# One tile of rows in every three rounds fetched by SyncE, row by row, and left out of GpSimd's gathers

## The reference

```
s, v = x[:, :64], x[:, 64:].reshape(n, 32, 3)
h_s, h_v = (s @ lin1_ws) * a / 8, einsum('nci,cd->ndi', v, lin1_wv) * a / sqrt(32)
w = silu(edge_scalars @ fc_w1 / 8) @ fc_w2 / 8            # 224 weights an edge
w1..w5 = split(w);  es, ev = h_s[edge_src], h_v[edge_src]  # the gather
messages = products of w1..w5, es, ev and the 4 edge attributes
agg = segment_sum(messages, edge_dst) / 4
out = layernorm(x + gated(sc(x) + lin2(agg)))
```

## Time and profile before

| | us |
|---|---|
| median of 3 runs | 3984.4 (3984.01 to 3986.15) |
| the profiled execution | 3985.22 |
| its span | 3983.4 |
| PE busy | 3715.0 (93%) |
| POOL busy | 2965.0 (74%) |
| DVE busy | 2438.8 (61%) |
| ACT busy | 2019.7 (51%) |

### The profile page before, as it was taken

One profiled execution on the slowest core, in us unless ns is written; L12 is line 12 of the kernel. 1 busy time (PEld: TensorE's weight loads), 2 busy tenths in 40 slices (PEclk: granted clock), 3 DMA queues, 4 the chain that ended last, 5 costly groups with the idle time before them and its releaser, 6 DMA issues.

```text
span 3983.4 us, 63960 instructions
## 1 busy us (share of the span) xinstructions
PE 3715.0 (93%) x18692; PEld 1572.6 (39%) x18692; DVE 2438.8 (61%) x7711; ACT 2019.7 (51%) x5186; POOL 2965.0 (74%) x3149
## 2 busy tenths in 40 slices
PE   7999999999999999999999999999999999999998
PEld 5344433433333433333333333333333333333333
DVE  6666666666656665666666666666666666666665
ACT  3455545554545455545555555555554545454554
POOL 5777777777777777777777777777777777777775
PEclk8999999999999999999999999999999999999999
DMA  7644444444444444444444444444444444444443
GB/s 270 184 131 130 127 127 120 129 123 127 121 126 123 127 123 127 124 127 122 128 122 128 122 128 122 127 122 126 124 123 126 123 127 122 128 121 127 122 128 101
DMA packets 367409, 516.31 MB, mean 130 GB/s; under 512 B 67378, under 2 KB 246266, under 8 KB 366942
## 3 DMA queue, kind: packets, MB, share of 16 engines
q0 software_dynamic: 150384, 256.47, 25.6%
q10 hardware_dynamic: 164522, 180.81, 15.2%
q1 hardware_dynamic: 52164, 75.02, 6.0%
HBM read 431.97 MB, written 80.06 MB: 129 GB/s over the span
## 4 chain that ended last, share of the span: by engine, by line
POOL 45%; PE 21%; issue 16%; DMA 9%; DVE 7%; ACT 0%; ACTq 0%; DVEq 0%; SPq 0%
POOL rows L888 45%; DMA rows<-h_table,src_cols 8%; PE psw L1245 7%; PE pst_e L1253 6%; DVE prod L732 5%; PE psg L1266 2%; PE psg L1264 2%; PE psx L1237 2%; DVE prod L743 1%; DVE prod L742 1%; DMA agg_table<-aggsb 1%; PE psx L1289 0%; PE psx L1274 0%; DMA es<-in_esP 0%; PE psw L1289 0%
## 5 line engine op out<-in xcount | busy, mean ns | idle before, releaser
L888 POOL DMA_INDIRECT rows<-h_table,src_cols x3093 | 2924.2, 945 | 975.9 <-issue 932.4
L732 DVE TENSOR_TENSOR prod<-psw,rows 128x384 f32<-128x384 f32 (+2 forms) x3128 | 1213.0, 450 | 1449.1 <-DMA rows<-h_table,src_cols 1112.3
L1245 PE MATMUL psw<-fc,hid 128*128 128x448 f32 x3128 | 1399.1, 570 | 1.4 <-ACT hid L939 1.4
L949 ACT ACTIVATE aggsb<-psg 32x160 f32<-32x160 f32 x3128 | 920.8, 294 | 558.6 <-PE psg L1266 524.1
L1264 PE MATMUL psg<-tsum,shifts 128*64 128x320 f32 x3126 | 1008.9, 445 | 1.0 <-ACT tsum L973 1.0
L1253 PE MATMUL pst_e<-prod,sel 128*32 128x448 f32 x6256 | 753.6, 554 | 233.7 <-DVE prod L743 231.1
L1266 PE MATMUL psg<-tsum,shifts 128*64 128x288 f32 x3126 | 926.1, 419 | 0.0
L1245 PEld LDWEIGHTS psw<-fc,hid 128*128 128x128 f32 x3128 | 535.8, 191 | 872.5 <-issue 864.3
L1264 PEld LDWEIGHTS psg<-tsum,shifts 128*64 128x64 f32 x3126 | 363.9, 136 | 432.2 <-issue 354.3
L973 ACT ACTIVATE tsum<-pst_e 128x448 f32<-128x448 f32 x782 | 424.8, 543 | 180.8 <-PE pst_e L1253 164.6
L939 ACT ACTIVATE hid<-psx 128x512 f32<-128x512 f32 x391 | 233.6, 597 | 557.6 <-PE psx L1237 541.2
(11 more groups left out here) (168 smaller groups left out, 1345.8 us busy)
## 6 DMA issues: line engine op xcount, KB each, us to landing
es<-in_esP ACTq DMA_DIRECT2D x391, 256.0 KB
agg_table<-aggsb ACTq DMA_DIRECT2D x782, 80.0 KB
rows<-h_table,src_cols POOLq DMA_INDIRECT x3093
nag<-agg_table SPq DMA_DIRECT2D x96, 320.0 KB
nxin<-in_xN SPq DMA_DIRECT2D x96, 208.0 KB
h_table<-e_cols ACTq DMA_DIRECT2D x24, 320.0 KB, 5.7
out<-yn SPq DMA_DIRECT2D x95, 80.0 KB
e_cols<-in_xaT SPq DMA_DIRECT2D x24, 256.0 KB, 7.9
```

What stands on the lines that cost most here:

```text
L732: return nc.vector.tensor_tensor(out, w_part, ev, ALU.mult)
L888: nc.gpsimd.indirect_dma_start(out=rows[:, p * QT + j, :], out_offset=None, in_=m.h, in_offset=bass.IndirectOffsetOnAxis(ap=m.src[:, t:t + ...
L949: ins = nc.scalar.activation(aggsb[r, b, :], joined(psg[r, :], k), ACT.Copy)
L1245: ins = nc.tensor.matmul(psw[b][:, 2 * c:2 * c + 2, 0:WN], hid[:, at:at + P], m.fc2[:].rearrange("p (t w) -> p t w", t=2)[:, :, 0:WN], sta ...
```

## The change

In 90 of the rounds (3 to 92, fifteen trips of six rounds), SyncE brings in one tile in every three rounds: the last tile of quad 8(3k + 7) + 7, for k = 0 to 29, so quads 63, 87, ..., 759. GpSimd issues three gathers instead of four for such a quad, 30 fewer in all (3063).

For each such tile SyncE loads the tile's 128 indices into SBUF (`fidx`, from a new input `srcR` that holds the indices by tile), reads them eight at a time into registers, and issues one DMA for each of the 128 rows, from `h_table` to one partition of a separate buffer (`fetched`, two of them). The 128 are spread over three rounds: 24 and 16 of them, 24 and 24, 24 and 16, the first part between the round's node loads and its store, the second behind the store. Then it waits for all 128, and for the place to be free, and copies the buffer into the ring with one DMA (`hand_over`), about fifteen quads before the quad is due. VectorE waits for that copy (`handed`) besides the three gathers. Rounds 93 on, and round 2, run as before on SyncE.

```
+AHEAD = RING
+TRIP = 3
+TRIPS = (ROUNDS - 3) // (2 * TRIP)
+def fetched_quad(k):
+    return RING * (TRIP * k + 7) + RING - 1
+FETCHED = [fetched_quad(k) for k in range(2 * TRIPS)]
+def gathered(q):
+    if q < AHEAD:
+        return 0
+    return LAST_REAL if q == QUADS - 1 else QT - (q in FETCHED)
+BATCH = 8
+FETCH_ROWS = [(0, 24, 40), (40, 64, 88), (88, 112, P)]
...
+        fetched = [sb(f"fetched{b}", [P, F]) for b in range(2)]
+        fidx = sb("fetch_indices", [1, P], I32)
...
             def round_of(R, quads, loading, storing):
-                if loading:
-                    sp.wait_ge(agg_stored[0], 16 * ((RING // 2) * R + 1))
-                    sp.sem_inc(loads_seen, 1)
-                    node_load(R - 2, P, main, 0, storing)
+                node_begin(R, loading, storing)
...
+            def fetch_indices(k, first):
+                if not first:
+                    sp.wait_ge(prod_ready, fetched_quad(k - 2) + 1)
+                    sp.sem_inc(loads_seen, 1)
+                sp.dma_start(fidx[:], io["srcR"][ds(fetched_quad(k) * QT + QT - 1, 1), :]).then_inc(fetch_idx, 16)
+                sp.wait_ge(fetch_idx, 16 * (k + 1))
+                sp.sem_inc(loads_seen, 1)
+            def fetch(b, first, last):
+                for at in range(first, last, BATCH):
+                    sp.load(places, fidx[0:1, at:at + BATCH])
+                    for n in range(BATCH):
+                        node = sp.snap(places[n], min_val=0, max_val=N - 1)
+                        sp.dma_start(fetched[b][at + n:at + n + 1, :], m.h[ds(node, 1), :]).then_inc(fetch_rows[b], 16)
+            def hand_over(k, b, trip):
+                p = FETCHED[b] % PLACES
+                sp.wait_ge(fetch_rows[b], 16 * P * (trip + 1))
+                sp.sem_inc(loads_seen, 1)
+                sp.wait_ge(prod_ready, fetched_quad(k) - PLACES + 1)
+                sp.sem_inc(loads_seen, 1)
+                sp.dma_start(rows[:, QT * p + QT - 1, :], fetched[b][:]).then_inc(handed[b], 16)
+            def trip_of(trip, first):
+                for b in range(2):
+                    k = 2 * trip + b
+                    for r in range(TRIP):
+                        R = 3 + TRIP * k + r
+                        node_begin(R, True, True)
+                        if r == 0:
+                            fetch_indices(k, first)
+                        fetch(b, FETCH_ROWS[r][0], FETCH_ROWS[r][1])
+                        node_store(R - 3, P, main)
+                        fetch(b, FETCH_ROWS[r][1], FETCH_ROWS[r][2])
+                    hand_over(k, b, trip)
...
-                with sp.Fori(3, ROUNDS) as R:
+                trip_of(0, True)
+                with sp.Fori(1, TRIPS) as trip:
+                    trip_of(trip, False)
+                with sp.Fori(3 + 2 * TRIP * TRIPS, ROUNDS) as R:
                     round_of(R, RING, True, True)
...
                 for q in range(AHEAD, QUADS):
-                    for j in range(QT if q < QUADS - 1 else LAST_REAL):
+                    for j in range(gathered(q)):
                         gather(q, j, freed(q) if j == 0 else 0)
...
-                    dve.wait_ge(rows_loaded[p], 16 * (QT * (q // PLACES - (p < AHEAD)) + tiles))
+                    dve.wait_ge(rows_loaded[p], 16 * sum(gathered(n) for n in range(p, q + 1, PLACES)))
+                if q in FETCHED:
+                    dve.wait_ge(handed[FETCHED.index(q) % 2], 16 * (FETCHED.index(q) // 2 + 1))
```

More of the change, by code:

```diff
@@ L39 @@
 PLACES = 2 * RING
+AHEAD = RING
[10 more added lines that the diff above has]
+FETCH_ROWS = [(0, 24, 40), (40, 64, 88), (88, 112, P)]
+assert FETCHED[-1] < ROUNDS * RING and 2 * TRIP * RING % PLACES == 0
 LOOSE = 12 * RING
@@ L76 @@
 HCHUNKS = NBLK // CB
-AHEAD = RING
 XBEFORE = [9, 11, 13, 15, 17, 19, 21, 23]
@@ L676, in edge_block @@
         rows_loaded = [sem(f"rows_loaded{p}") for p in range(PLACES)]
+        fetch_idx = sem("fetch_indices_loaded")
+        handed = [sem(f"handed_over{b}") for b in range(2)]
+        fetch_rows = [sem(f"fetched_rows{b}") for b in range(2)]
         pad_cleared = sem("pad_cleared")
@@ L822, in round_of, with node_begin @@
                     node_store(R - 3, P, main)
+            def node_begin(R, loading, storing):
+                if loading:
+                    sp.wait_ge(agg_stored[0], 16 * ((RING // 2) * R + 1))
+                    sp.sem_inc(loads_seen, 1)
+                    node_load(R - 2, P, main, 0, storing)
+            places = [sp.alloc_register(f"source{n}") for n in range(BATCH)]
+            def fetch_indices(k, first):
[16 more added lines that the diff above has]
+                sp.wait_ge(prod_ready, fetched_quad(k) - PLACES + 1)
+                sp.sem_inc(loads_seen, 1)
+                sp.dma_start(rows[:, QT * p + QT - 1, :], fetched[b][:]).then_inc(handed[b], 16)
[11 more added lines that the diff above has]
+                    hand_over(k, b, trip)
             def load_sources():
@@ L1438 @@
         "xg": np.concatenate([xT.T, np.asarray(node_vec1).reshape(N, 1)], axis=1),
+        "srcR": src.reshape(TILES, P),
         "quad_base": tile_base.reshape(QUADS, QT).T,
```

## The result

| | before | changed |
|---|---|---|
| median, us | 3985.28 (4 runs, 3984.01 to 3986.55) | 3947.55 (4 runs, 3947.21 to 3948.70) |
| span of the profiled execution, us | 3983.4 | 3946.9 |

The ratio is 0.9906, with a 95% interval of 0.9895 to 0.9918: 37.7 us less. The forecast was 3946.9 us.

What follows compares the result with a forecast made beforehand. GpSimd's gathers, 1.250 us each, were taken to set the pace; 30 fewer save 37.5 us with nothing deducted for the fetches: 3984.4 - 37.5 = 3946.9 us. The range 3943 to 3976 us was given 0.80.

Steps and rivals of the forecast that it cites:

- GpSimd's part: On GpSimd, 30 gathers fewer at 1.250 us save 37.5 us, all on the path, if three covers hold.
- First cover: GpSimd's wait on `tiles_summed` before a shortened quad's gathers: 4.95 us to spare, so no loss counted.
- the 4.95 us to spare: Margin at gather 1545, first of quad 394, between the 392nd quad's sums ending at 2010.48 us and its start at 2015.43.
- Third cover: GpSimd's step of 1.250 us a gather stays despite the fetches' DMA traffic; 18 to 28 us on one engine, nothing deducted.
- SyncE's part: SyncE's room for 128 DMAs a tile: 105 us of 118.8 for three rounds, between 93 and 147, at 0.64 us a row.
- the sign I had named: In the changed profile, SyncE's 3840 one-row DMAs would be 0.59 to 0.70 us from start to start.
- Late node loads: On SyncE, the middle round's 24 rows behind the store overrun 15.0 us; next loads 3.1 us late, some 7 to spare.
- Rival 1: SyncE becomes the bound through the 128 DMAs, from 0.75 us a row on; 4490 us at 0.86; chance 0.13.
- Rival 2: Node loads 6 us late make TensorE stand, losing 0.7 us in each of 30 trips: 3968 us; chance 0.10.
- Rivals 3 and 4: Third: GpSimd's step grows 12 ns, 3984 us, chance 0.05; fourth: fetches serial on one DMA engine, about 9200 us, 0.02.

Runs made afterwards that it cites:

- GpSimd's part alone: Changed kernel without SyncE's fetches: GpSimd leaves the 30 tiles out and their products use old rows; ratio 0.9906 to the kernel before.
- late_48: Changed kernel with 48 rows fetched behind the store of the first of three rounds and fewer elsewhere; ratio 1.0135 to the kernel before.
- every_two_rounds: Changed kernel with one tile fetched in every two rounds, 46 tiles instead of 30; ratio 1.0113 to the kernel before.
- rows_twice: Changed kernel with each of the 128 rows fetched twice, the second time into a buffer nobody reads; 4187.0 us in one run.
- the two halves: Changed kernel split: GpSimd omits 30 tiles, nobody fetches them (0.9906); SyncE fetches into an unread buffer, GpSimd gathers everything (1.0002); ratios to the kernel before.
- the lighter version: every_two_rounds with indices read 16 at a time and loaded a tile ahead, 48 rows before the store, 16 behind; ratio 0.9857 to the kernel before.

## Why the prediction was right

- *GpSimd's part.* 30 x 1.250 us was the whole effect: 37.5 expected, 37.7 measured, and GpSimd's part alone gives the same ratio. Reading GpSimd as the bound from its waits, against busy shares of 74% and 93%, was the step that decided.
- *First cover, its wait on sums.* No wait over 0.3 us, as said. But the cover is thinner than I made it. I read the 4.95 us to spare at a single gather, and left out that a TensorE that has stood also runs at half clock for a while (late_48). The first gather of quad 148 in the changed kernel, number 557, waits for 146 summed quads. The sums of the 146th and this gather, in the timeline:

```profile
778.09 0.96 PE L1328 MATMUL pst_e<-prod,sel 128*32 128x448 f32 x8
...
779.63 0.94 POOL L961 DMA_INDIRECT rows<-h_table,src_cols  x1 [0.30 <-issue]
```

That is 0.58 us to spare. Before it TensorE was busy 2.77 of the 5 us from 760 to 765, and from 765 to 770 its granted clock was 0.66. Of the 343 gathers that wait in this way, 21 have under 3 us to spare in the changed kernel, and 17 in the kernel before, with 1.16 us as the least. So it held, but at its thinnest place by half a microsecond.
- *Third cover, the step of 1.250 us.* It stayed. The packets are as I had assumed there, two a fetch: 64224 - 52164 = 12060 packets more on SyncE's queue are 3840 x 2 for the fetches, 30 x 144 for the copies and 30 x 2 for the indices. By size, the trace of that queue has 7680 more packets of 640 bytes, 30 of 512 and 4350 of 4 bytes, so one of each kind a fetch, and 128 and 16 a copy. The Trainium skill states in "DMA: Bandwidth & Descriptors" ("Why a DMA increments its semaphore by 16 and not by 1") that each engine that takes part in a DMA ends it with a write to the semaphore. The trace agrees with that, if the packets of 4 bytes are these writes: a fetch then ran on one engine and a copy on sixteen. That all fetches used the same engine no row shows. They cost less than I took: (6.5% x 3946.9 - 6.0% x 3983.4) x 16 / 12060 = 0.023 us each, 6 us a tile and not 18 to 28.
- *SyncE's part* was mis-sized. A row costs 0.418 us from start to start (2000.182 to 2000.600 us in the trace, 228 ns of it the DMA), not 0.64, and less than my lower bound of 0.59: I took SyncE's 333 ns for a DMA of 128 rows as the least, and a DMA of one row is cheaper; what lies between two of them is 0.19 us and not 0.26. The loads were 0.78 us where I said 0.9. The sum I put at 105 us of 118.8, and at 93 at the least, is 75.4 + 5 = 80. So the sign I had named, 0.59 to 0.70 us from start to start, did not appear. The error was on the safe side here, since SyncE had room either way; a version on the edge (every_two_rounds) is decided by such a sum, and there I erred the other way.
- *Late node loads.* I expected the middle round's to be 3.1 us late; at 0.418 us a row they were not late at all.
- *Rival 1* needs 0.75 us a row. The fetches cost 0.42, far from it. rows_twice, at 0.74 for a pair, is over the edge already and 202 us slower, since the waits and gaps between the parts count as well: the edge lay nearer than 0.75.
- *Rival 2* did not occur, but its price was wrong in kind: the loss does not start where TensorE starts to stand but where standing and slow clock together pass what GpSimd has to spare, and then it is 3 us a time at a stop of 4.7 us.
- *Rivals 3 and 4* are excluded by the two halves and by SyncE's wait for its last row: 38.2 us in 30, 1.3 us each, after 128 DMAs issued 0.42 us apart.

## What to carry to other kernels

When an engine is bound by issuing, look for the engine whose queue waits, and price the moved work by what that engine's waits lose, not only by the sum of its instructions: by the parts, 70 us a tile, 46 tiles seemed to have 5 us of room in two rounds, by the waits, 75.4 us, they had none, and that version lost 45 us. Where the idle engine has steps that others depend on, place the new work ahead of the step that has slack (here the store) and leave what is to spare before the one that has not (the node loads): late_48 does the same work as the changed kernel in another order and is 91 us slower. And read what a wait has to spare at many places, not at one: 4.95 us at the gather I chose, 0.58 at the worst.

## What the runs showed of the hardware that I had not expected

- A DMA of one 640-byte row takes SyncE 228 ns to issue, a node load over 128 partitions 333 to 365, and the copy of 128 rows from SBUF to SBUF 517. Reading eight indices into registers takes 0.78 us, and sixteen 1.24 (line 870 of the lighter version, 1138/1237/1793 ns), so the larger batch saves a fifth of it.
- In a stop of TensorE of 4.70 us the granted clock falls, and it is still 0.50 when TensorE works again, here from 2080 to 2085 us, busy for all of it; from 2085 on it is 1.00.
- GpSimd's step of 1.250 us for a gather of 128 rows did not change with 3840 more DMAs on another queue, nor with the DMA engines at 65% (late_48, 2075 to 2080 us) instead of 46%.
